# A state-space scan whose loop over sequences is written out, with the residual added two positions later

## The reference

```
xz = layernorm(x) @ in_proj^T ;  x', z = split(xz)              # 512 channels each
u = silu(causal_conv(x', 4 taps) + conv_b)
dt, B, C = split(u @ x_proj^T)                                  # 64, 16, 16
delta = softplus(dt @ dt_proj^T + dt_b) ;  A = -exp(A_log)
h[t] = h[t-1] * exp(delta[t] * A) + (delta[t] * u[t]) * B[t]    # 512 channels x 16 states
y[t] = sum over states (h[t] * C[t]) + D * u[t]
x1 = x + (y * silu(z)) @ out_proj^T
```

## Time and profile before

| | |
|---|---|
| runs | 6872.57, 6882.47, 6873.41 us, median 6873.41 |
| profiled execution | 6878.51 us, of which the span is 6876.8 us |
| granted TensorE clock, mean of the span | 0.948 |
| busy, share of the span | TensorE 88%, GpSimd 77%, VectorE 60%, ScalarE 51% |
| costliest group on GpSimd | L373, 1024 multiplications, 2395.0 us, 2369 ns each |
| costliest group on VectorE | L634, 2048 scans, 2459.1 us, 1210 to 1274 ns each |
| end of the state-space stage | last scan starts at 3760.0 us |

### The profile page before, as it was taken

One profiled execution on the slowest core, in us unless ns is written; L12 is line 12 of the kernel. 1 busy time (PEld: TensorE's weight loads), 2 busy tenths in 40 slices (PEclk: granted clock), 3 DMA queues, 4 the chain that ended last, 5 costly groups with the idle time before them and its releaser, 6 DMA issues. The chain is left out here.

```text
span 6876.8 us, 90070 instructions
## 1 busy us (share of the span) xinstructions
PE 6057.5 (88%) x24804; PEld 3848.5 (56%) x24804; DVE 4131.6 (60%) x4999; ACT 3516.7 (51%) x6417; POOL 5285.1 (77%) x4084
## 2 busy tenths in 40 slices
PE   7999989998989998999897899930299999999999
PEld 3444434443434443444443688830288888888888
DVE  6999999989999999999998477750000000000000
ACT  6676667666666666666665688720022222222222
POOL 6999999999999999999998777637655555555554
PEclk9999999999999999999999999965699999999999
DMA  3554555555554554455554244410266666666654
GB/s 124 163 161 161 159 160 161 157 153 163 160 161 156 160 163 157 157 162 160 161 158 142 73 123 125 125 60 1 76 183 183 184 184 184 185 185 185 180 168 132
DMA packets 556960, 1030.16 MB, mean 150 GB/s; under 512 B 82546, under 2 KB 250996, under 8 KB 521904
## 3 DMA queue, kind: packets, MB, share of 16 engines
q1 hardware_dynamic: 441168, 669.34, 31.4%
q0 software_dynamic: 115296, 355.56, 17.5%
HBM read 926.04 MB, written 88.88 MB: 148 GB/s over the span
## 5 line engine op out<-in xcount | busy, mean ns | idle before, releaser
L373 POOL TENSOR_TENSOR m_dbu<-m_du,m_bb 128x1024 f32<-128x1024 f32 x1024 | 2395.0, 2369 | 55.3 <-DVE m_h L634 54.6
L751 PE MATMUL m_y_bank<-m_prod,m_ident 128*128 128x512 f32 x4096 | 1955.6, 606 | 157.2 <-POOL m_prod L382 153.8
L524 ACT ACTIVATE m_decay<-m_delta,m_a_neg 128x512 f32<-128x512 f32 x2048 | 1417.6, 694 | 916.0 <-DVE m_h L634 893.5
L751 PEld LDWEIGHTS m_y_bank<-m_prod,m_ident 128*128 128x128 f32 x4096 | 778.4, 193 | 1125.9 <-issue 900.5
L634 DVE TENSOR_TENSOR_SCAN m_h<-m_decay,m_dbu 128x512 f32<-128x512 f32 x1024 | 1198.2, 1210 | 107.3 <-issue 76.9
L634 DVE TENSOR_TENSOR_SCAN m_h<-m_decay,m_h_end,m_dbu 128x512 f32<-128x512 f32 x1024 | 1261.0, 1274 | 0.7
L1694 DVE TENSOR_SCALAR e_ye<-e_ybank,e_listing 128x256 f32<-128x256 f32 x270 | 118.3, 480 | 1818.7 <-PE e_ybank L1728 1818.7
L1680 ACT ACTIVATE e_a<-e_ubank 128x512 f32<-128x512 f32 x540 | 322.4, 597 | 1474.9 <-PE e_ubank L1719 1474.9
L382 POOL TENSOR_TENSOR m_prod<-m_h,m_cb 128x1024 f32<-128x1024 f32 x416 | 983.8, 2365 | 90.5 <-DVE m_h L634 83.2
L1719 PE MATMUL e_ubank<-e_xT,e_w 128*128 128x256 f32 x4320 | 979.5, 380 | 1.3 <-ACT e_xT L1671 1.3
L1728 PE MATMUL e_ybank<-e_w,e_a 128*128 128x256 f32 x4320 | 954.5, 379 | 0.7 <-ACT e_a L1680 0.7
(11 more groups left out here) (198 smaller groups left out, 6532.1 us busy)
## 6 DMA issues: line engine op xcount, KB each, us to landing
m_bb<-rows_bc SPq DMA_DIRECT2D x1024, 256.0 KB, 3.7
m_cv<-rows_bc SPq DMA_DIRECT2D x608, 256.0 KB, 3.8
m_cb<-rows_bc SPq DMA_DIRECT2D x416, 256.0 KB, 3.4
m_xin<-in_x SPq DMA_DIRECT2D x32, 512.0 KB, 5.4
m_xres<-in_x SPq DMA_DIRECT2D x32, 512.0 KB, 5.5
x<-m_xres SPq DMA_DIRECT2D x32, 512.0 KB, 6.0
a_xa<-x SPq DMA_DIRECT2D x64, 256.0 KB, 2.9
a_xr<-x SPq DMA_DIRECT2D x64, 256.0 KB, 3.2
```

Of the source, the lines that this page charges most:

```text
L373: nc.gpsimd.tensor_tensor(dbu[:, slot], du[:, q[1], p * PC:(p + 1) * PC], bb[:, slot].unsqueeze(1).to_broadcast([P, PC, T]), ALU.mult).the ...
L524: nc.scalar.activation(decay[:, cc], delta[:, r, c], ACT.Exp, scale=a_neg[:, c, n:n + 1]).then_inc(decay_done, 1)
L751: ins = nc.tensor.matmul(y_bank[:, cc], ident[:], prod[:, slot, cc], start=False, stop=(n == NS - 1))
```

## The change

`sequences` becomes a loop of Python: the body is written out 16 times on each of the five engines. The register arithmetic goes, and so do the jumps. `wait_apart` goes, and its three users call `wait`. `add_residual` is called at `filled_at.get(v - TAKE)`, that is three positions behind the filling, at 45 and 50 in place of 43 and 48.

```diff
 def wait(eng, sem, value):
 
-    if isinstance(value, int) and value <= 0:
+    if value <= 0:
         return
     eng.wait_ge(sem, value)
-
-
-def wait_apart(eng, sem, value, passed):
-
-    if isinstance(value, int) and value <= 0:
-        return
-    eng.wait_ge(sem, value)
-    eng.sem_inc(passed, 1)
...
         def sequences(eng, body):
 
-            body(0, False)
-            with eng.Fori(1, S - 1) as b:
-                body(b, False)
-            body(S - 1, True)
+            for b in range(S):
+                body(b, b == S - 1)
...
             def wait_then(sem_, value):
-                wait_apart(sp, sem_, value, sp_passed)
+                wait(sp, sem_, value)
...
-                wait_apart(act, prep_taken, count(q, PREPS, prep_done("dt", i)), act_passed)
+                wait(act, prep_taken, count(q, PREPS, prep_done("dt", i)))
...
-                wait_apart(dve, stats_done, count(q, 2, 1), dve_passed)
+                wait(dve, stats_done, count(q, 2, 1))
...
-                if outs and filled_at.get(v - 1) in out_uses:
-                    add_residual(before(q), filled_at[v - 1][1])
+                if outs and filled_at.get(v - TAKE) in out_uses:
+                    add_residual(before(q), filled_at[v - TAKE][1])
```

More of the change, by code:

```diff
@@ L187, in mamba_stage @@
         s_diag = sem("diag")
-        dve_passed, sp_passed = sem("dve_passed"), sem("sp_passed")
-        act_passed = sem("act_passed")
         x_loaded = sem("x_loaded")
@@ L230, in first @@
         def first(q):
-            return isinstance(q[0], int) and q[0] == 0 and q[1] == 0
+            return q == (0, 0)
         def sequences(eng, body):
-            body(0, False)
-            with eng.Fori(1, S - 1) as b:
-                body(b, False)
-            body(S - 1, True)
+            for b in range(S):
+                body(b, b == S - 1)
         def unit_at(q, u):
```

## The result

The changed kernel takes **6726.7 us** (median of 4 runs, 6724.0 to 6729.4), the kernel before 6875.4 us on the same chip. The ratio is 0.9782, with a 95% interval of 0.9765 to 0.9799. The forecast was 6729 us.

What follows compares the result with a forecast made beforehand. GpSimd was taken as the floor, with VectorE's lateness on top. The profiled 6878.5 us less 141.2 us (sequences 1 to 14) and 3.4 us gave 6733.9 us; with the median 5.1 us lower, 6729 us, range 6708 to 6792 us.

Steps and rivals of the forecast that it cites:

- The floor: Sequences 1 to 14 of the state-space stage: GpSimd's 3246.7 us less 150.2 us of waits for VectorE, 3096.5 us.
- The jump and not the seam: VectorE's 7.4 us stalls at thirteen loop starts belong to the jump back, not to the seam between two sequences.
- GpSimd's 4.10 us: GpSimd's wait at 533.78 us, behind a jump: what comes through of VectorE's 7.4 us stall, as GpSimd runs ahead.
- 87.9 us for the loop: Jumps' worth in sequences 1 to 14: GpSimd's 150.2 us of waits less 62.3 us, from the first pass's 4.45 us.
- The cross-check by lengths: Loop passes: twelve of 232.4 us each against the last of 224.5 us, 8 us per jump, 104 us for thirteen.
- 56.7 us for the residual on top: Residual at positions 45 and 50: VectorE's 66.4 us of waits go, GpSimd's remaining 62.3 us falls to 9 us.
- the signs of being right: No VectorE issue wait over 1 us, no residual wait, GpSimd's waits under 20 us, stage end near 3617 us.
- Case 2: Only the jumps' share comes, GpSimd's small waits stay: 6785 us, chance 0.20; half the jump's gain lost too: 6829 us, 0.07.
- Case 3: The jump is not the cause, the seam keeps its stall and only the residual acts: 6838 us, chance 0.04.
- Case 4: Slower, as straight code must be fetched and stalls: 6959 us with two stalls per half, chance 0.05.
- The margin of 1.5 us for TensorE's second bank: VectorE takes the second output piece at some 1315.6 us, TensorE refills its bank at 1317.81 us: cost zero.
- The parts outside: Three halves with a residual outside sequences 1 to 14 (one of sequence 0, two of 15): 1.1 us each, together 3.4 us.

Runs made afterwards that it cites:

- two-sequence pass: Kernel before with the residual moved as in the changed kernel and two sequences per loop pass, so 6 jumps back in place of 13: 6767.3 us.
- one-pass loops: Against the changed kernel, each of sequences 1 to 14 in a loop of its own that runs once, branches kept, none going back: 6743.1 us.

## Why the prediction was right

**The floor.** 3096.5 us by GpSimd for fourteen sequences, plus 9 us of waits left: 3105.5 us. Measured 3106.1 us. The waits left are 13.3 us, and GpSimd's busy time stayed as it was, 3088.4 us against 3091.0.

**The jump and not the seam.** Right as put, from two seams without a stall. The two-sequence pass shows it directly, and the kernels with the loop on some engines show VectorE's own jump as the one that counts. That GpSimd's 4.10 us of the earlier trace rows came from VectorE and not from its own jump was in the row's name for the releaser. My expectation for the loop on the other four engines forgot this, and lay 36 to 86 us too high.

**87.9 us for the loop.** Measured 89.9. The price rests on the loop's first pass, the one place in the old trace that ran the same work with no jump in front. The cross-check by lengths, 104 us, was further off. It took the last pass alone, 224.5 us, as the length without a jump. In the written-out kernel with the old residual the fourteen sequences last 225.3 us each, 7.1 us less than the 232.4 of the twelve passes, and 13 x 7.1 = 92 us.

**56.7 us for the residual on top** (144.6 less 87.9). Measured 57.8. The argument by what VectorE has in hand from one half to the next held: the waits near 74 us into a half, which lie ahead of the residual, went too, down to 0.74 us and 0.2 us. Less sure is the room that the sum gave VectorE, 0.9 us per sequence under GpSimd "with its other waits kept". Those waits grew from 55.0 to 84.2 us, and they are no room to spare: when VectorE got 1.1 us more work per half and GpSimd less, they shrank by 3.3 us only, and the kernel became slower. One of the signs of being right, no "issue" wait over 1 us, failed with them, by fourteen waits of 1.3 us before a product.

**Case 2 (6785 us)**, the jumps' share only, is the time of the written-out loop without the residual's move (6784.4), but as a forecast of the whole it was wrong: the later residual brought what was claimed. **Case 3 (6838 us)** was ruled out, and its price was 16 us too high, since the kernel with only the residual moved takes 6822. **Case 4**, stalls in straight code, shows nowhere: GpSimd's longest wait is 0.8 us.

**The branch's price.** The Trainium skill (Advanced Engine Details and Errata, Control Flow Timing) gives 108 ns for a compare-and-branch. The one-pass loops agree that the instruction itself is cheap: its row lasts 0.03 to 0.09 us there, and their seams have no gap. The stall of a jump back, 4.0 to 8.3 us on VectorE here, has to be added to it. It agrees with what the Trainium skill (Runtime: NRT & Kernel Launch) says under Instruction fetch mechanics of a taken branch whose target is no longer in the window. The evidence here is that q14 fetched code again on each pass, and that GpSimd's and TensorE's sequencers go on at once behind a jump over 266 and 1154 instructions and stand 3.4 to 5.3 us behind one over 528 and 2296. With them go the packets behind VectorE's jumps. No run changes the fetch alone, so that it is the whole of the stall is argued, though no row speaks against it.

**Off by size.** The margin of 1.5 us for TensorE's second bank was read as tight. It was not: even at five positions TensorE waits 1.5 us in all of fourteen sequences. "The parts outside" were put at 3.4 us. They brought 9.4 us within the stage (2.4 before the first scan, 2.9 in sequence 0, 4.2 in sequence 15), and 4.5 us lie behind it.

**The total is closer than the sum deserves.** The sum for the profiled execution was 6733.9 us, and it took 6724.0: a gain of 154.5 us, where 144.6 were forecast. The difference lies outside the fourteen sequences, 13.9 us in place of 3.4. The forecast of 6729 then took off 5.1 us because the profiled execution before lay above its median; the one after lay 2.7 us below its median. That 6729 and 6726.7 differ by 2.3 us is luck; the parts for the fourteen sequences, 141.2 us forecast and 140.6 measured, are not.

## What to carry to other kernels

A hardware loop whose body is long can cost an engine a stall at its jump back. Which engines it costs depends on the length of each one's own body, and what counts is the stall of the engine that has nothing in hand. Look for a pass without a jump in front: here it priced the loop at 87.9 us, and 89.9 were measured. A wait that one in-order engine has for a late bank can be removed by taking the bank a few positions later, here at no cost for three positions and for five. How many positions it takes depends on how far ahead that engine runs. When two engines are within 1% of each other, moving work from the one to the other makes the kernel slower by what the second has to do more: 37 us here, for 31 products of 1.1 us.

## What the runs showed that I had not expected

- The same jump costs engines differently: VectorE stands idle 4.1 to 5.3 us with itself alone in the loop, ScalarE at most 2.6 us, GpSimd not at all. VectorE's stall grows to 5.7 to 7.1 us when all five jump, and does not with ScalarE or TensorE alone as partner. GpSimd's and TensorE's sequencers stand too once their bodies are twice as long.
- TensorE's granted clock goes with single microseconds on other engines. Where a wait of 3 us at the start of a half is followed by a clock of 0.70 instead of 0.83 to 1.00 over 10 us, in both halves, the sequence is 4 us longer, in VectorE's waits for TensorE at the gate and for `decay`.
- Fourteen sequences of the changed kernel agree within 0.1 us, while kernels with a nearly equal program (one-pass loops, loops on four engines) have three or four of fourteen that are 4 us longer. Why is open.
